# PSUM banks of a gated cross-attention layer: three for the transposed scores and two for the spare uses, in place of two and three

## The chip, the cores and the metric

The kernel runs on one core of one Trainium2 chip. The metric is the device time of one execution in microseconds (us), as the median of several executions. The engines are called TensorE (PE in the profile, with PEld for its weight loads), VectorE (DVE), ScalarE (ACT), GpSimd (POOL) and SyncE (SP, which issues most of the DMAs). PSUM, into which TensorE writes, has eight banks of 512 fp32 columns, and the kernel uses all of them.

## What is computed

One layer: gated cross-attention of 8 sequences of 112 queries on 375 context rows each, then a gated mixture of 8 feed-forward experts of which each sequence takes 3.

```
q = layernorm(x) @ Wq + bq; k = ctx @ Wk + bk; v = ctx @ Wv + bv      # 16 heads of 16
s = where(mask, -1e15, q k^T / 4); a = softmax(s) @ v; y = a @ Wo + bo
x = x + tanh(g_xattn) * y
n = layernorm(x)
p = softmax(tanh(mean(n, 1) @ W1 + b1) @ W2 + b2); w = the top 3 of 8, divided by their sum
z = n + sum over the 8 experts e of w[e] * gelu(n @ Wa[e]) @ Wb[e]
x = x + tanh(g_ffn) * z
```

## The kernel before

The engines run programs of their own, which meet in semaphores only. The attention stage is one loop over b from -2 to 7 (for TensorE lines 1244 to 1257), a pipeline over sequences: in pass b the sequence b gets its exponentials and its product with v, sequence n = b+1 its row maxima and v, sequence m = b+2 its context transposes, q and k, sequence o = b-1 its output projection, and sequence b-2 its second layernorm. After the loop comes the feed-forward stage (24 units u, three for each sequence, functions g1 and g2, lines 1267 to 1322).

A pass has four slots. In each, TensorE's program is

```python
st_tile(b, slot, 0)
s1(b + 1, 2 * slot)
st_tile(b, slot, 1)
pv(b if slot else b - 1, (slot - 1) % COUPLES)
...
st_tile(b, slot, 2)
s1(b + 1, 2 * slot + 1)
for name in uses[len(first):]:
    put(name)
```

- **st_tile(b, g, c)** (lines 1072 to 1088) computes one tile of transposed scores, keys by queries of four heads, in the bank `ST_BANKS[t % len(ST_BANKS)]` for tile number t. It is one matmul at line 1081 (maximum and mask) and two at line 1085. First it waits until the exponential of tile t - len(ST_BANKS) is done (line 1076). ScalarE's exp_tile (lines 547 to 555) reads the bank and writes pT, a ring of five tiles, for which it waits until the product pv that read the old tile is done.
- **s1(b, p)** (lines 1062 to 1070) computes the scores of two heads in banks 0 and 1 (line 1069), from which VectorE's row_max (lines 799 to 809, the instruction at line 807) takes maxima. At the first and the fifth pair it waits for q and k, which SyncE reads back from DRAM (lines 321 to 343).
- **pv(b, g)** (line 1101) multiplies by v into bank 5, and waits for the exponentials of tile (b, g, 2).
- **put(name)** is one of the spare uses, the small products of which there are 7 to 14 in a pass from b = 0 on. They take the spare banks in turn (class Spare, lines 89 to 122), and `use` (lines 1052 to 1057) waits until whoever read the last use of the same bank is done (table FREED, lines 78 to 86).

The spare uses of a full pass (2 to 5), in TensorE's order (slot_uses, lines 62 to 72):

| slot | ahead of st_tile(b, slot, 2) | behind it |
|---|---|---|
| 0 | MX1 of b, CX0 and CX1 of m | XT of m, OT of o, K0 of m |
| 1 | | K1 and Q of m, X2T of b-2 |
| 2 | MX0 of n | V0 of n, ON of o |
| 3 | | V1 of n, OP of o |

MX (line 1163) transposes row maxima, and ScalarE's max_copy (line 632) frees its bank. CX (line 1110) transposes the context; ScalarE frees CX0 (line 639) and VectorE CX1 (line 843). K0 and K1 (line 1119) are the projection of k: ScalarE's k_hi (line 655) and then VectorE's k_lo (line 849) read it, and k_lo frees the bank. Q (line 1145) is done in the same way (lines 647 and 857). X2T (line 1192) transposes the second layernorm's result: ScalarE's x2_hi (line 582) and then VectorE's x2_lo (lines 893 and 894) read it, and the last of these frees the bank; in VectorE's program x2_lo stands behind row_max(n, 5). V0 and V1 (line 1128) are the projection of v, read by ScalarE's v_copy (line 615). OT (line 1170), ON (line 1177) and OP (line 1185) belong to the output projection. X2T and what follows from it are missing where b-2 is below 0, and CX, XT, K and Q where b+2 is above 7.

ScalarE's order in a pass (lines 682 to 732) mixes these copies with the exponentials, and ends each slot with two instructions w_hi (line 665), which convert parts of the feed-forward weights; GpSimd follows them with lo_part (line 474), and only then may SyncE load further parts (lines 353 to 365) into the ring `stage`. GpSimd scales the parts that have landed (line 469) and computes the reciprocal deviation of the second layernorm (norm2, lines 479 and 480) in between; ScalarE's normed2 (line 604) waits for it, and the exponentials of slot 1 stand behind normed2 on ScalarE. SyncE's order in slot 2 is: the transposed maxima (line 350, behind max_copy of MX0), a load of weights, then k and q of m read back (lines 341 and 329).

Of the kernel before, what the change touches and what calls it, by code (L numbers as in the profile page):

```python
# [37 lines left out]
PRING = 5  # L38
ROUTES = ((0, B - 3), (B - 3, 3))
VC = HD + 1  # L40
ST_BANKS = (2, 3)
O_BANK = 5
MISC_BANKS, TAIL_BANKS = (4, 6, 7), (6, 7)


def parts_at(b, slot):
# [90 lines left out]
def need(eng, sem, n):  # L137
    if n > 0:
        eng.wait_ge(sem, n)


def flamingo_layer(nc, x, ctx, mask, g_xattn, g_ffn, Wq, bq, Wk, bk, Wv, bv, Wo, bo,
                   W1, b1, W2, b2, Wa, Wb, out):
    with ExitStack() as stack:
# [119 lines left out]
        def tile(b, g, c):  # L264
            return (b * COUPLES + g) * KC + c
# [269 lines left out]
        def _(act):  # L535
# [11 lines left out]
            def exp_tile(b, g, c):  # L547

                if there(b):
# [3 lines left out]
                    if t == 0:  # L553
                        act.wait_ge(s["zeroed"], 5)
                    a.activation(pT[0:CK, t % PRING, :], bank[0:CK, ST_BANKS[t % len(ST_BANKS)], 0:QUAD], ACT.Exp).then_inc(s["act_exp"], 1)  # L555

# [491 lines left out]
        def _(pe):  # L1048
# [23 lines left out]
            def st_tile(b, g, c):  # L1072

                if there(b):
                    t = tile(b, g, c)
                    need(pe, s["act_exp"], t - len(ST_BANKS) + 1)
                    o = bank[:, ST_BANKS[t % len(ST_BANKS)], 0:QUAD]
                    w = 128 if c < KC - 1 else CK
# [269 lines left out]
```

## Time and profile before

| | |
|---|---|
| median of 3 executions | 325.48 us (325.46 to 325.75) |
| the profiled execution | 328.27 us, its span 326.4 us |
| attention stage | up to 202.4 us of the span |
| feed-forward stage | the last 124 us |
| TensorE busy | 287.3 us, 88% of the span |
| mean granted clock of TensorE | 0.979 of full speed |

The span is what the trace covers; 1.9 us of the profiled execution lie around it. Times of rows are microseconds from the start of the span. The profiled execution took 2.8 us more than the median one.

### The profile page before, as it was taken

What the parts mean: (1) busy time and instruction counts of PE and PEld (TensorE: products, weight loads), DVE (VectorE), ACT (ScalarE), POOL (GpSimd) and SP (SyncE); (2) the same over time, 40 slices, a digit from 0 to 9 for tenths busy, and PEclk for the clock granted to TensorE, in tenths of its full rate; (3) what the DMA queues carried; (4) which work ended last, traced back from release to release, by engine and by line L of the source; (5) the groups of instructions that cost most, each with busy time, mean ns of one, the idle gap of its engine ahead of it and who ended that gap; (6) DMA issues with size and microseconds to landing.
All of it is one profiled execution on the core that took longest, in us unless ns stands there. A gap on an engine that the chain in (4) does not pass through costs nothing.

```text
span 326.4 us, 10356 instructions
## 1 busy us (share of the span) xinstructions
PE 287.3 (88%) x3940; PEld 238.6 (73%) x3940; DVE 225.3 (69%) x642; ACT 223.1 (68%) x439; POOL 135.4 (41%) x185
## 2 busy tenths in 40 slices
PE   1808769899989999999998977899999999999996
PEld 1505546667756776767765646799999989999996
DVE  7326846657757797777867626876976877686773
ACT  2221456786958968789687674986866977766863
POOL 3401274876768968689677983000100000000000
PEclk9967989999999999999999999999999999999999
DMA  7457667686777778866686322100201011010101
GB/s 166 120 125 239 156 176 213 167 241 172 233 182 216 206 230 230 264 177 172 207 217 208 88 87 80 38 19 16 58 17 46 3 44 37 11 45 3 32 2 30
DMA packets 39457, 40.59 MB, mean 124 GB/s; under 512 B 10264, under 2 KB 35264, under 8 KB 39408
## 3 DMA queue, kind: packets, MB, share of 16 engines
q1 hardware_dynamic: 37296, 38.94, 42.5%
q10 hardware_dynamic: 1936, 0.79, 1.0%
q8 instruction: 32, 0.52, 0.7%
q0 software_dynamic: 176, 0.20, 0.2%
q14 instruction: 17, 0.14, 0.1%
HBM read 33.09 MB, written 6.74 MB: 122 GB/s over the span
## 4 chain that ended last, share of the span: by engine, by line
PE 63%; DMA 12%; ACT 7%; issue 6%; DVE 5%; SPq 4%; POOL 3%; DVEq 0%; ACTq 0%
PE bank L1280 16%; PE bank L1307 16%; PE bank L1119 7%; PE bank L1128 5%; PE bank L1069 4%; DMA qbd<-q_scr 4%; PE bank L1081 4%; DMA stage<-in_L_ffn_Wb 4%; PE bank L1085 3%; PE bank L1101 2%; ACT pT L555 2%; PE bank L1110 2%; PE bank L1145 2%; DMA ctx_s<-in_ctx 2%; POOL wa L474 1%
## 5 line engine op out<-in xcount | busy, mean ns | idle before, releaser
L807 DVE CUSTOM_DVE_ANT_0 bank<-bank,maskb 112x375 f32<-112x375 f32 x128 | 67.9, 571 | 42.1 <-PE bank L1069 42.1
L1280 PE MATMUL bank<-ctxT,wqkvo 128*128 128x112 f16 x960 | 59.4, 213 | 2.7 <-DVE qbd L933 2.3
L1280 PEld LDWEIGHTS bank<-ctxT,wqkvo 128*128 128x128 f16 x960 | 56.5, 98 | 3.4 <-issue 3.4
L1307 PE MATMUL bank<-stage,pT 128*128 128x112 f16 x1104 | 58.1, 213 | 0.0
L1307 PEld LDWEIGHTS bank<-stage,pT 128*128 128x128 f16 x1104 | 55.8, 98 | 0.3
L555 ACT ACTIVATE pT<-bank 125x448 f32<-125x448 f32 x96 | 49.0, 540 | 9.9 <-PE bank L1085 9.3
L469 POOL TENSOR_SCALAR stage<-stage 128x512 f32<-128x512 f32 x64 | 38.5, 620 | 27.4 <-DMA stage<-in_L_ffn_Wa 20.6
L1069 PE MATMUL bank<-kst,qbd 128*112 128x375 f16 x128 | 33.7, 338 | 16.0 <-DMA qbd<-q_scr 12.7
L474 POOL TENSOR_TENSOR wb<-stage,wb 128x512 f16<-128x512 f32 x32 | 37.6, 1195 | 14.5 <-ACT wb L665 14.4
L1081 PE MATMUL bank<-rq,maskb 115*128 115x448 bf16 (+1 forms) x96 | 35.5, 370 | 8.3 <-ACT pT L555 7.8
L474 POOL TENSOR_TENSOR wa<-stage,wa 128x512 f16<-128x512 f32 x32 | 36.4, 1158 | 10.8 <-ACT wa L665 10.8
L1280 PE MATMUL bank<-ctxT,qbd 128*128 128x112 f16 x192 | 40.8, 213 | 0.0
L754 ACT ACTIVATE pT<-wb 128x1024 f16 x23 | 24.3, 1056 | 15.4 <-PE bank L1307 13.3
L1085 PE MATMUL bank<-qbd,kst 128*128 128x224 f16 (+1 forms) x192 | 34.4, 260 | 0.0
L932 DVE COPY wqkvo<-wa 128x3072 f16 x24 | 23.4, 973 | 15.6 <-PE bank L1280 14.2
L744 ACT ACTIVATE stage<-kst,wbc 128x448 f16<-128x448 f32 x48 | 32.1, 668 | 1.6
L1006 DVE SCALAR_TENSOR_TENSOR stage<-kst,wbc,stage 128x448 f16<-128x448 f32 x48 | 32.6, 679 | 0.6 <-ACT stage L744 0.6
L944 DVE COPY pT<-wb 128x3072 f16 x23 | 22.1, 959 | 12.5 <-PE bank L1307 12.5
L1085 PEld LDWEIGHTS bank<-qbd,kst 128*128 128x128 f16 (+1 forms) x192 | 21.6, 113 | 11.8 <-issue 1.3
L1069 PEld LDWEIGHTS bank<-kst,qbd 128*112 128x112 f16 x128 | 14.8, 132 | 21.0 <-DMA qbd<-q_scr 13.9
L742 ACT ACTIVATE kst<-bank 128x448 f32<-128x448 f32 x48 | 25.5, 532 | 2.8 <-PE bank L1280 2.8
L479 POOL TENSOR_TENSOR rstd<-ve,half 112x1 f32<-112x1 f32 x16 | 8.8, 551 | 39.8 <-DVE ve L829 39.8
(134 smaller groups left out, 480.2 us busy)
## 6 DMA issues: line engine op xcount, KB each, us to landing
stage<-in_L_ffn_Wa SPq DMA_DIRECT2D x16, 512.0 KB, 4.5
stage<-in_L_ffn_Wb SPq DMA_DIRECT2D x16, 512.0 KB, 4.5
kst<-k_scr SPq DMA_DIRECT2D x64, 93.8 KB, 3.6
k_scr<-wb SPq DMA_DIRECT2D x16, 187.5 KB
ctx_s<-in_ctx SPq DMA_DIRECT2D x8, 336.0 KB
qbd<-q_scr SPq DMA_DIRECT2D x32, 56.0 KB, 3.0
xa<-in_x SPq DMA_DIRECT2D x8, 112.0 KB, 4.1
q_scr<-wb SPq DMA_DIRECT2D x16, 56.0 KB, 3.3
```

Of the source, the lines that this page charges most:

```text
L469: g.tensor_scalar(st, st, WSCALE, 1.0, ALU.mult, ALU.mult).then_inc(s["scaled"], 1)
L474: g.tensor_tensor(part_dst(k, 1), stage[:, k % RING, :], part_dst(k, 0), ALU.subtract).then_inc(s["lo_done"], 1)
L555: a.activation(pT[0:CK, t % PRING, :], bank[0:CK, ST_BANKS[t % len(ST_BANKS)], 0:QUAD], ACT.Exp).then_inc(s["act_exp"], 1)
L742: a.activation(h_w[:, cols], bank[:, 2 * (u % 2) + hf, 0:QUAD], ACT.Gelu_apprx_tanh, scale=1.0 / WSCALE).then_inc(s["gelu_done"], 1)
L744: a.activation(hT[:, u % 2, cols], h_w[:, cols], ACT.Copy, scale=wbc[:, u:u + 1]).then_inc(s["hthi_done"], 1)
L807: v.tensor_tensor_reduce(out=bank[0:SQ, e, 0:SK], in0=bank[0:SQ, e, 0:SK], in1=maskb[0:SQ, b % 2, 0:SK], scale=-1.0, scalar=FLOOR, op0=ALU ...
L1006: v.scalar_tensor_tensor(out=hT[:, u % 2, (2 + hf) * QUAD:(3 + hf) * QUAD], in0=h_w[:, cols], scalar=wbc[:, u:u + 1], in1=hT[:, u % 2, col ...
L1069: T.matmul(bank[0:SQ, e, 0:SK], qbd[:, b % 2, e, p, :], kst[:, b % 2, p * SK:(p + 1) * SK], start=True, stop=True).then_inc(s["pe_s1"], 1)
L1081: T.matmul(o[0:w, :].rearrange("k (j q) -> k j q", j=4), maskb[0:KQ, b % 2, c * CK:c * CK + w], rq[0:KQ, g // 2, :, g % 2, :], start=True, ...
L1085: ins = T.matmul(o[0:w, i * 2 * SQ:(i + 1) * 2 * SQ].rearrange("k (e q) -> k e q", e=2), kst[:, b % 2, p * SK + c * CK:p * SK + c * CK + w ...
L1280: ins = T.matmul(o, first(ws, t, f), x2b[:, b % 2, (xs * DT + t) * SQ:(xs * DT + t + 1) * SQ], start=(t == 0 and xs == 0 and ws == 0), sto ...
L1307: ins = T.matmul(o, second(u, ws * (2 * CHUNK) + f * D + t * 128), hT[:, u % 2, hs * FT * SQ + f * SQ:hs * FT * SQ + (f + 1) * SQ], start= ...
```

## The change

The bank 7 moves from the spare uses to the transposed scores. Two constants are all that is edited. `st_tile` and `exp_tile` take the number of banks from the length of ST_BANKS, so tile t now waits for the exponential of tile t - 3 and the bank is the same as c; Spare deals the uses of the loop to the banks 4 and 6 in turn, so each waits for the use two before it, no longer for the one three before it. The uses behind the loop keep the banks 6 and 7.

```diff
-ST_BANKS = (2, 3)
+ST_BANKS = (2, 3, 7)
 O_BANK = 5
-MISC_BANKS, TAIL_BANKS = (4, 6, 7), (6, 7)
+MISC_BANKS, TAIL_BANKS = (4, 6), (6, 7)
```

What each use of a full pass waits for, by FREED, in the two versions (the kind of use whose reader frees the bank; "last" is the pass before):

| use | before | after |
|---|---|---|
| MX1 | ON, last | V1, last |
| CX0 | V1, last | OP, last |
| CX1 | OP, last | MX1 |
| XT | MX1 | CX0 |
| OT | CX0 | CX1 |
| K0 | CX1 | XT |
| K1 | XT | OT |
| Q | OT | K0 |
| X2T | K0 | K1 |
| MX0 | K1 | Q |
| V0 | Q | X2T |
| ON | X2T | MX0 |
| V1 | MX0 | V0 |
| OP | V0 | ON |

In pass 6, X2T waits for MX1 after the change and V0 for X2T; in passes 0 and 1, which have no X2T, V0 waits for Q.

## Rows read from the trace of the kernel before

**Rows 1.** TensorE's waits: engine, line, released by, us in total, times, longest.

```profile
PE bank L1069 <- DMA qbd<-q_scr: 12.7, 4, 8.3
PE bank L1081 <- ACT pT L555: 7.8, 13, 1.6
```

**Rows 2.** A stretch of 20 us: busy PE, PEld, DVE, ACT, POOL; clock; DMA share; GB/s.

```profile
109.00:129.00 20.00, 19.11 (x188) 14.01 (x176) 15.52 (x58) 16.18 (x38) 16.08 (x22) 1.00 0.77 225
```

**Rows 3.** Timeline of TensorE in pass 3: start us, us, engine, line.

```profile
109.25 0.86 PE L1110 MATMUL bank<-ident,ctx_s 125*128 125x125 f32 x6
109.95 0.35 PE L1081 MATMUL bank<-rq,maskb 115*125 115x448 bf16 x1
...
117.41 0.36 PE L1192 MATMUL bank<-ident,x 112*128 112x112 f32 x2
...
119.74 0.40 PE L1081 MATMUL bank<-rq,maskb 115*125 115x448 bf16 x1
...
120.50 1.89 PE L1128 MATMUL bank<-wqkvo,ctxT 128*125 128x256 f32 x8
...
124.89 0.40 PE L1081 MATMUL bank<-rq,maskb 115*125 115x448 bf16 x1 [0.37 <-ACT pT L555]
...
128.33 0.53 PE L1069 MATMUL bank<-kst,qbd 128*112 128x375 f16 x2 [0.42 <-DMA qbd<-q_scr]
```

**Rows 4.** Timeline of ScalarE in pass 3.

```profile
109.56 0.33 ACT L632 ACTIVATE ms<-bank 12x224 bf16<-12x224 bf16 x1
...
116.73 0.58 ACT L655 ACTIVATE wb<-bank,bk_c 128x375 f16<-128x375 f32 x1 [1.04 <-PE bank L1119]
...
122.43 0.69 ACT L615 ACTIVATE vp<-bank,vsc 125x512 f32<-125x512 f32 x1 [1.27 <-PE bank L1128]
...
124.29 0.98 ACT L555 ACTIVATE pT<-bank 125x448 f32<-125x448 f32 x2
```

**Rows 5.** Timeline of VectorE in pass 3.

```profile
117.34 0.61 DVE L849 SCALAR_TENSOR_TENSOR wb<-bank,bk_c,wb 128x375 f16<-128x375 f32 x1
...
120.53 0.56 DVE L807 CUSTOM_DVE_ANT_0 bank<-bank,maskb 112x375 f32<-112x375 f32 x1 [0.29 <-PE bank L1069]
...
121.81 0.38 DVE L894 TENSOR_REDUCE pooled<-bank 128x2 f32<-128x224 f32 x1
```

**Rows 6.** Pass 5: TensorE's CX0 and CX1 (six transposes), ScalarE's max_copy.

```profile
150.05 0.86 PE L1110 MATMUL bank<-ident,ctx_s 125*128 125x125 f32 x6
...
150.28 0.33 ACT L632 ACTIVATE ms<-bank 12x224 bf16<-12x224 bf16 x1
```

**Rows 7.** TensorE, longer waits of st_tile(b, 1, 2) in passes 2, 6 and 7.

```profile
94.39 0.40 PE L1081 MATMUL bank<-rq,maskb 115*125 115x448 bf16 x1 [1.56 <-ACT pT L555]
...
174.76 0.40 PE L1081 MATMUL bank<-rq,maskb 115*125 115x448 bf16 x1 [0.86 <-ACT pT L555]
...
193.17 0.40 PE L1081 MATMUL bank<-rq,maskb 115*125 115x448 bf16 x1 [1.36 <-ACT pT L555]
```

**Rows 8.** Pass 2: ScalarE's exponentials of slot 1, TensorE's X2T. Pass 6: V0, x2_lo's end.

```profile
93.81 0.96 ACT L555 ACTIVATE pT<-bank 125x448 f32<-125x448 f32 x2
...
97.28 0.36 PE L1192 MATMUL bank<-ident,x 112*128 112x112 f32 x2
...
179.59 0.60 PE L1128 MATMUL bank<-wqkvo,wb 128*125 128x256 f32 x2
...
180.56 0.38 DVE L894 TENSOR_REDUCE pooled<-bank 128x2 f32<-128x224 f32 x1
```

**Rows 9.** The chain that ended last, from 180 us on: start us, us, what.

```profile
183.05 2.28 POOL wa L474 x2
...
185.35 4.65 DMA stage<-in_L_ffn_Wb
...
192.60 0.53 ACT pT L555
...
197.95 4.13 DMA ctxT<-x_scr
```

## The prediction, made before the run

> **What bounds the kernel.** I read the chain that ended last first, then TensorE's waits, the busy times by stretch, and last the timelines of three engines through one pass. From 205 us on the chain is almost all TensorE in the feed-forward stage, where the change touches nothing: its banks and its spare uses are the old ones. So all is decided in the attention stage. There TensorE is busy 19.11 of 20 us in pass 3 [rows 2]: whatever it waits more, it loses, and what it waits less it wins. Its waits in the whole kernel [rows 1] name what the change aims at: 7.8 us at line 1081, st_tile waiting for ScalarE's exponential to give a score bank back. The 12.7 us for q and k from DRAM lie mostly in the first passes, before the uses have a queue. No row of before shows a wait at a spare use for its bank. With three banks that price is hidden, so it must be worked out from when each reader finishes.
>
> A semaphore from reader to TensorE costs about 0.06 us: in slot 3 of pass 3 the first of two exponentials begun at 124.29 [rows 4] (0.98 together, 0.54 the second, begun 0.44 after the first) ends near 124.83, and st_tile goes at 124.89 [rows 3].
>
> **What the third score bank gives.** In pass 3, st_tile(3, 3, 2) waited 0.37 for an exponential that stood behind weight conversions [rows 3]. That tile now needs one computed a slot earlier, so the wait goes. st_tile(3, 2, 2) at 119.74 was late by some 0.12 too, in the same way. This repeats in passes 4 and 5: a gain of 0.49 each. Longer waits stand at st_tile(b, 1, 2) in passes 2, 6 and 7: 1.56, 0.86 and 1.36 [rows 7], where ScalarE was held by the second layernorm. What is late next there is X2T, which needs that layernorm's result as well. So these go only in part (below).
>
> **What two spare banks cost.** I compare each use's start with the end of the reader that it newly waits for, in pass 3. Eleven of the fourteen find their bank free, as their readers end 0.2 us or more before, or are waited for anyway; these I cost at nothing, and what hides them is the slot of TensorE work between. Three don't:
> - CX1, the second three of six transposes issued from 109.25 to 109.95 [rows 3], would start at 109.60. MX1, just ahead, is read by ScalarE until 109.89 [rows 4], and it can't be read sooner, as two exponentials stand before it. Wait: 109.89 + 0.06 - 109.60 = 0.35. In pass 5 [rows 6] 150.61 + 0.06 - 150.40 = 0.27; I take 0.27 for pass 4 as well and 0.2 for pass 1.
> - X2T started at 117.41 [rows 3]. K1's readers are k_hi, 116.73 to 117.31 [rows 4], and k_lo, 117.34 to 117.95 [rows 5]. Wait: 117.95 + 0.06 - 117.41 = 0.60. Only Q stands between K1 and X2T and both readers follow K1 at once, so this moves with TensorE and can't be caught up. Queued behind are st_tile(b, 2, 0) and the fifth pair's scores; VectorE has other work there.
> - V0 started at 120.50 [rows 3]. Its bank is now freed by x2_lo, which VectorE ends at 121.81 + 0.38 = 122.19 [rows 5], since it stands behind row_max(n, 5), begun at 120.53 as soon as the scores arrive [rows 5]. Wait: 122.19 + 0.06 - 120.50 = 1.75. This too moves with TensorE: VectorE was idle 0.29 before that maximum. Behind V0 stand ON, the next tiles and, on ScalarE, v_copy at 122.43 [rows 4] with all that follows it: the copy of ON, two weight conversions and three exponentials. Before, V0's 1.8 us of matmuls covered x2_lo, and ON was the one to wait for it; the cover is gone.
>
> One wait for a transfer goes in return: s1 at 128.33 waited 0.42 for q [rows 3]; TensorE comes there later now, and the read doesn't move as far.
>
> **The sum.** Pass 3: 0.35 + 0.60 + 1.75 - 0.49 - 0.42 = +1.8. Passes 4 and 5: 0.27 + 0.60 + 1.75 - 0.49 = +2.1 each. Pass 1: +0.2; it has no X2T, and what its st_tiles gain in slots 2 and 3 is held back by the read of q, which follows MX0 by 8 to 9 us. Pass 0 the same, taken as nothing. Pass 2: the exponentials of slot 1 start at 93.81 [rows 8] whatever happens, as ScalarE waits for GpSimd; now the three run in a row, 0.44 apart, to 95.2, then k_hi (0.58) and k_lo (0.61) with two hops give 96.5, and X2T, which was at 97.28 [rows 8], moves 0.8 forward. CX1's 0.25 is swallowed there. Then + 1.75 - 0.49: +0.5. Pass 6: slot 1 gains about 0.8 of its 0.86 at V0, and V0 would wait 180.94 + 0.06 - 179.59 = 1.4 [rows 8]: +0.6. From V0 of pass 6 on the chain leaves TensorE: ScalarE's conversion, GpSimd (from 183.05), a load of weights of 4.65 us, the scaling, the second layernorm, the exponentials at 192.60, the routing, and the read at 197.95 that starts the feed-forward stage [rows 9]. It carries over what V0 lost, and gains 0.3 since the third exponential of slot 1 no longer waits for its tile. TensorE's 1.36 in pass 7 [rows 7] is beside that chain and worth nothing. Sum: 0.2 + 0.5 + 1.8 + 2.1 + 2.1 + 0.6 - 0.3 = +7.0 us. The profiled execution would go from 328.3 to 335.3; it stands 2.8 above the median of 325.5, so the median goes to 332.5.
>
> Bounds of what no row shows. V0's wait: at the least 1.4 per pass (the row of pass 6), at the most 1.75 and 0.5 more if ScalarE's share of x2 comes late; I take 1.75, from the nearest rows, four of five passes being alike. The hop: 0.02 to 0.1. The CX1 wait: 0 if ScalarE runs ahead, 0.5 if V0's delay leaves it behind. The gains: all 7.8 us at the upper end.
>
> **Rivals.**
> - *The bubbles are the bound, and the spare banks are not* (faster). The 7.8 us at line 1081 [rows 1] come off in full and the three waits are covered by work that I don't see. If a third of them, 3, remained: 325.5 - 7.8 + 3 = 320.7. For it: it is the only wait for a PSUM bank that the profile shows, at the same place in each pass. Against it: 3.8 of the 7.8 are the rows 7, held by the layernorm, and V0's reader ended 1.7 after V0's start in each pass. The Trainium skill, in Perfetto Trace Analysis, section Optimization Strategy, says that a gap which repeats on the engine that should be saturated can mean too little PSUM for the next tile. By that rule this rival would come true; the repeated gap of 0.37 is there, but it is the smaller of the two prices. It decides for itself if V0 finds its bank free.
> - *The transfers of q and k set the period* (slower, less). MX0 at about 119.4 releases, by SyncE's order, the read that s1 waited for at 128.33. Then only what lies ahead of MX0 counts, CX1 and X2T, and V0's wait hides beside the transfer: 5 passes by about 0.7, or +3.5: 329.0. Against it: that wait was 0.42 in pass 3 and next to nothing in the others, so it hides 1.75 nowhere.
> - *ScalarE becomes the bound* (slower still). V0's delay moves v_copy, conversions and, through GpSimd and the weight loads, the second layernorm. The holes of rows 7 then open in passes 3 to 5 too, as waits of pv or X2T: 3 by about 1.2, 7.0 + 3.6 = 10.6: 336.1. For it: ScalarE has 16.18 of 20 us of work in the pass [rows 2]. Against it: it idles 1.27 right before v_copy and 1.04 before k_hi [rows 4].
> - *Nothing is to be seen*: gains and losses cancel, 325.5. It needs V0's wait at 0.3.
>
> **How the numbers follow.** About 0.2% is what a measurement of this kernel can tell from no change. The forecast gets 0.68, with a range of its own from 330 to 334.8. The transfers get 0.11, ScalarE 0.10, the bubbles 0.08, nothing 0.03. Range: 328.8 to 335.4, which takes in the forecast, the transfers' rival and the near end of ScalarE's; the rest is left out. Faster: 0.08; same 0.03; slower 0.89.
>
> **What would show it.** In TensorE's waits, line 1081 falls from 7.8 to below 1, and new rows appear: line 1128 waiting for VectorE's line 894, 5 times, 8 us in all; line 1192 for line 849, 3 or 4 times, 2 us; line 1110 for ScalarE's line 632, 0.2 to 0.4 each. The passes 3 to 5 last 22 to 23 us instead of 20 to 21, and the feed-forward stage is as long as before and starts 7 us later. I am wrong if V0 starts right behind the sixth pair's scores, if a pass is not longer, or if VectorE or ScalarE show waits that were filled before.

## The result, and the profile after

The changed kernel takes 337.13 us (median of 4 executions) against 325.62 for the kernel before: a ratio of 1.033, 95% interval 1.023 to 1.042. It is slower, as forecast, but by 11.5 us where 7.0 was forecast, and above the range (335.4). The executions fall into two groups, two at 334.8 and 335.1, two at 339.2 and 340.0, and the median lies in the gap between them; the next runs show what parts them. The profiled execution, 334.82 us with a span of 332.9, is one of the lower group.

TensorE's waits after the change (engine, line, released by, total us, times, longest):

```profile
PE bank L1069 <- DMA qbd<-q_scr: 12.5, 4, 8.4
PE bank L1128 <- DVE pooled L894: 8.2, 5, 1.7
...
PE bank L1216 <- DVE pooled L894: 2.7, 1, 2.7
PE bank L1110 <- ACT ms L632: 2.3, 4, 0.7
...
PE bank L1192 <- DVE wb L849: 2.1, 4, 0.5
```

Line 1081, with 7.8 us the second row of [rows 1], is gone from the list. In its place stand the three waits of the forecast: V0 (line 1128) five times, X2T (line 1192) four times, CX1 (line 1110). A fourth was not forecast: W (line 1216) in pass 7 waits 2.7 us for x2_lo.

The same places of pass 4 in the timeline of TensorE, and ScalarE's max_copy and the first layernorm ahead of it, which answer to [rows 3, 4, 6]:

```profile
130.76 0.54 PE L1110 MATMUL bank<-ident,ctx_s 125*128 125x125 f32 x3
131.96 0.54 PE L1110 MATMUL bank<-ident,ctx_s 125*128 125x125 f32 x3 [0.66 <-ACT ms L632]
...
140.75 0.38 PE L1192 MATMUL bank<-ident,x 112*128 112x112 f32 x2 [0.52 <-DVE wb L849]
...
145.54 1.96 PE L1128 MATMUL bank<-wqkvo,wb 128*125 128x256 f32 x8 [1.69 <-DVE pooled L894]
...
149.41 0.40 PE L1081 MATMUL bank<-rq,maskb 115*125 115x448 bf16 x1
```

```profile
130.23 0.60 ACT L596 ACTIVATE xa<-xa,nmr,rstd 112x256 f32<-112x256 f32 x1 [0.58 <-POOL nmr L480]
130.73 0.96 ACT L555 ACTIVATE pT<-bank 125x448 f32<-125x448 f32 x2
131.58 0.33 ACT L632 ACTIVATE ms<-bank 12x224 bf16<-12x224 bf16 x1
```

V0 and X2T cost what was worked out, 1.69 and 0.52. CX1 does not: its three transposes come 1.20 us after CX0's, where in the kernel before they come 0.35 after them, so it waits 0.85 and not 0.27 (the 0.66 of the row counts only from the end of CX0's). ScalarE is late for it because it waits 0.58 for GpSimd. The tile of slot 3, at 149.41, has no wait.

How long each pass lasts, from one MX1 to the next (line 1163, read from the timelines, in us), and the last stretch from MX1 of pass 7 to the first matmul of the feed-forward stage:

| kernel | 1 | 2 | 3 | 4 | 5 | 6 | last |
|---|---|---|---|---|---|---|---|
| before | 20.1 | 21.8 | 20.7 | 20.1 | 20.3 | 18.2 | 14.1 |
| changed | 19.9 | 22.7 | 23.1 | 23.1 | 23.1 | 18.2 | 14.3 |

The sum from pass 1 on is 9.2 us more, against 7.0 forecast. The traced execution of before was in addition 2.2 us later at MX1 of pass 0 (45.85 against 43.60). This is no effect of the change, as another traced execution of the changed kernel came there at 45.14: in all three traces TensorE's granted clock is at 0.50 early on, from 19 to 29 us in those two and from 20 to 27 us in this one. The 6.55 us between the two profiled executions hide that much of the loss.

### The profile page after: what moved, and what is told of

Its sections match the earlier page's. It is cut to its first block, busy times and chain, and to the rows that moved or that the text cites. A ratio compares the mean times of both kernels' runs of the same rounds, so it can differ in the third digit from the quotient of the medians.

```text
span 332.9 us, 10356 instructions
## 1 busy us (share of the span) xinstructions
PE 287.9 (86%) x3940; PEld 237.4 (71%) x3940; DVE 224.7 (67%) x642; ACT 222.2 (67%) x439; POOL 135.1 (41%) x185
## 4 chain that ended last, share of the span: by engine, by line
PE 61%; DVE 11%; POOL 6%; ACT 6%; DMA 5%; issue 5%; SPq 3%; ACTq 1%; DVEq 0%
PE bank L1280 16%; PE bank L1307 16%; PE bank L1119 6%; PE bank L1128 4%; DVE bank L807 4%; PE bank L1069 4%; PE bank L1081 4%; POOL wa L474 3%; PE bank L1085 3%; PE bank L1101 3%; DMA qbd<-q_scr 3%; PE bank L1110 2%; POOL stage L469 2%; DVE wb L849 2%; DMA k_scr<-wb 1%
## 5 line engine op out<-in xcount | busy, mean ns | idle before, releaser
L555 ACT ACTIVATE pT<-bank 125x448 f32<-125x448 f32 x96 | 47.8, 540 | 8.4 <-PE bank L1085 7.7
L469 POOL TENSOR_SCALAR stage<-stage 128x512 f32<-128x512 f32 x64 | 38.3, 617 | 25.5 <-DMA stage<-in_L_ffn_Wa 20.7
L1069 PE MATMUL bank<-kst,qbd 128*112 128x375 f16 x128 | 33.4, 336 | 15.2 <-DMA qbd<-q_scr 12.5
L932 DVE COPY wqkvo<-wa 128x3072 f16 x24 | 23.0, 960 | 15.2 <-PE bank L1280 13.8
L1069 PEld LDWEIGHTS bank<-kst,qbd 128*112 128x112 f16 x128 | 14.9, 132 | 19.3 <-DMA qbd<-q_scr 13.4
```

The source lines that it names most:

```text
L469: g.tensor_scalar(st, st, WSCALE, 1.0, ALU.mult, ALU.mult).then_inc(s["scaled"], 1)
L1069: T.matmul(bank[0:SQ, e, 0:SK], qbd[:, b % 2, e, p, :], kst[:, b % 2, p * SK:(p + 1) * SK], start=True, stop=True).then_inc(s["pe_s1"], 1)
```

## The experiments

They were run in three groups of four, each on a chip of its own with the kernel before beside it; its medians were 325.5, 325.4 and 326.5. The changed kernel itself was timed in the first group alone, so where a run of the other two is held against it, a difference between chips (1 us for the kernel before) is in the comparison.

**The changed kernel again.** No edit.

> The changed kernel as it is, timed again beside the kernel before. Four executions of it gave 334.8, 335.1, 339.2 and 340.0 us. Theory A (the lost 9 us are new waits at spare banks, and the 4 to 5 us above them in some executions are a clock level granted in a stretch): executions fall into two groups near 335 and near 339 to 340, and the longer ones show a mean granted clock lower by 0.010 to 0.015. Theory B (all of it is one effect that varies): times spread evenly between 334 and 341 at one clock. The kernel before stays at 325.5 to 326.

Median 339.30, ratio 1.039 (1.034 to 1.044); six executions: 334.9 and five from 338.6 to 339.9. So there are two groups, and the upper one is the usual one. With the first four executions, three of ten lie at 335. The profiled execution, of 339.93 us, had a mean clock of 0.970 against 0.985, and took 17.0 us for the last stretch of the table, where the one of the lower group took 14.3. From pass 1 on its sum is 147.8 us, against 144.4 there and 135.2 in the kernel before. Its end of pass 7, and under it that of the lower group (columns: the stretch, its length, busy PE, PEld, DVE, ACT, POOL, the granted clock, DMA share, GB/s):

```profile
200.00:208.00 8.00, 4.50 (x68) 2.86 (x66) 3.79 (x14) 4.94 (x13) 6.72 (x9) 0.93 0.12 31
208.00:214.00 6.00, 6.00 (x52) 3.60 (x55) 1.49 (x3) 1.63 (x3) 0.00 (x0) 0.53 0.34 100
```

```profile
198.00:206.00 8.00, 4.52 (x66) 2.82 (x55) 3.43 (x14) 4.93 (x13) 6.28 (x8) 1.00 0.16 42
206.00:209.00 3.00, 3.00 (x56) 2.06 (x57) 1.65 (x3) 1.52 (x3) 0.00 (x0) 1.00 0.44 130
```

Both had stood still for 2.7 us ahead of W. From W to the first matmul of the feed-forward stage the one takes 6.7 us (207.69 to 214.40) and the other 4.0 (205.25 to 209.21): the lower clock costs 2.8 us there. Theory A holds.

**Two score banks and two spare banks.** The loss without the gain.

```diff
-ST_BANKS = (2, 3, 7)
+ST_BANKS = (2, 3)
```

> Two score banks as before, but only the two spare banks of the change; bank 7 is left unused. This is the loss without the gain. Theory A (the third score bank gives what the waits at line 1081 were worth, about 3 us net of what slot 1 keeps): 3 to 4 us slower than the changed kernel, 338 to 339 at the fast level. Rival (the third score bank gives nothing, because what it advances waits again at a spare bank): within 1 us of the changed kernel. Second rival (ahead of V0's wait the score waits cost nothing any more): the same.

Median 340.62, ratio 1.045 (1.041 to 1.048): 1.3 us above the changed kernel, and not 3 to 4. Theory A misses, and the rivals' 1 us is passed by a little. In the traces the third score bank is worth 0.5, 0.7 and 0.7 us in passes 1, 2 and 6 (against the profiled execution of the run above), and nothing in passes 3 to 5: here st_tile waits again in slot 3,

```profile
129.03 0.40 PE L1081 MATMUL bank<-rq,maskb 115*125 115x448 bf16 x1 [0.51 <-ACT pT L555]
```

and yet passes 3 to 5 last 23.1 us each, just as with three score banks. In the changed kernel something else sets their length. In its chain of waits the stretch from one V0 to the next CX1 does not run through TensorE:

```profile
145.54 1.98 PE bank L1128 x8
147.54 0.22 ACT vp L615
...
148.47 0.53 ACT wa L665
...
149.07 2.29 POOL wa L474 x2
151.35 1.16 POOL stage L469 x2
152.52 0.52 POOL rstd L479
153.11 0.20 POOL nmr L480
...
153.84 0.62 ACT pT L555 x2
...
154.69 0.34 ACT ms L632
155.07 0.54 PE bank L1110 x3
```

V0, v_copy, a weight conversion on ScalarE, the subtraction and the scaling on GpSimd, the layernorm behind the scaling, two exponentials, max_copy, CX1; from there TensorE and VectorE lead to X2T and the next V0. The chain is closed, and a wait removed inside a slot of TensorE only makes CX1 wait longer. With two score banks it isn't this chain that binds: ScalarE has no wait at line 596 in passes 3 to 5, and CX0 and CX1 come as one group,

```profile
132.35 0.60 ACT L596 ACTIVATE xa<-xa,nmr,rstd 112x256 f32<-112x256 f32 x1
133.47 1.15 PE L1110 MATMUL bank<-ident,ctx_s 125*128 125x125 f32 x6
```

1.15 us long in place of the 0.86 of the kernel before, so that CX1 waits some 0.3, as forecast. There TensorE's own waits, 0.3, 0.5 for X2T and 1.7 for V0, make up nearly all of the 2.7 us by which the pass is longer than in the kernel before. That both ways come to 23.1 seems to be chance.

**V0 beside MX0.** Spare banks dealt by name: V0, OP, K0, Q, XT, CX0, MX0 on one bank, the others on the other, with exceptions in the first and last passes (W beside ON in pass 7, for one).

```diff
-                    banks.append(MISC_BANKS[len(names) % len(MISC_BANKS)])
+                    banks.append(MISC_BANKS[side(name[0], b)])
```

> Three score banks and two spare banks as in the change, but the spare uses are dealt by name, so that V0 takes the bank of MX0 and no longer that of X2T. V0 then waits for a copy that is done; the waits of CX1 and X2T stay. Theory A (V0's wait of 1.7 us in five passes is the main loss, and it also delays ScalarE's weight conversion, GpSimd, the layernorm and through it max_copy, which cost CX1 another 0.5 in four passes): 8 to 10 us come back, 325 to 328 us, CX1's wait falls from 0.66 to under 0.35, and the times no longer fall into two groups. Rival (V0's wait only takes the place of another, ON's or a transfer's): under 3 us come back, 332 or more.

Median 329.47, ratio 1.012 (1.009 to 1.015): 9.8 us less than the changed kernel beside it, as theory A had it, but 1.5 above the range given for the time. All six executions lie within 1.8 us, and their mean clocks are 0.974 to 0.979: the two groups are gone, the lower clock is not. In the trace it is at 0.50 from 194 to 197 us, behind a wait of X2T of 1.62 in pass 7. V0's wait is gone; W still waits 1.0, for ON's copy. X2T still waits 0.52 four times, CX1 0.65 and 0.47 in passes 2 and 3, 0.20 in pass 5, so that part of the expectation holds only in the later ones. Passes 1 to 6 take 121.8 us in all, against 130.1 and 130.7 in the two traces of the changed kernel and 121.1 in the kernel before. The edit deals every use anew, but V0's five waits, 8.2 us, are what is gone from the list, and they are the size of the gain in those passes: V0's bank was the main loss.

**X2T in slot 2.**

```diff
-        (("K1", m), ("Q", m), ("X2T", b - 2)),
-        (("MX0", n), ("V0", n), ("ON", o)),
+        (("K1", m), ("Q", m)),
+        (("X2T", b - 2), ("MX0", n), ("V0", n), ("ON", o)),
```

> As the run before, and X2T moves from the end of slot 1 to slot 2, ahead of MX0, where K1's readers have long been done. Theory A: X2T's wait of 0.5 us in four passes goes, 2 us less than the run with V0 alone: 322.5 to 326. Rival (MX0 now comes later behind X2T, the maxima and the transfers of q and k behind it too, and a wait for q returns): within 0.5 us of that run or slower.

Median 329.15, ratio 1.010 (1.006 to 1.014): 0.3 less, so as a time the rival holds, though not by its mechanism. X2T's wait is gone and passes 1 to 6 are 1.1 us shorter in all (120.7 against 121.8). The last stretch gave it back, 16.7 against 14.9: with X2T out of the way, TensorE stood in pass 7 in one piece for the exponential behind the second layernorm,

```profile
194.90 0.36 PE L1092 MATMUL bank<-rq,maskb 115*128 115x448 bf16 x1 [2.75 <-ACT pT L566]
```

and from 200 to 204 us its granted clock was 0.58, behind a second gap, of 1.82 ahead of W.

**W apart.** In the changed kernel, W of pass 7 on ON's bank and OP on that of X2T.

```diff
-                    banks.append(MISC_BANKS[len(names) % len(MISC_BANKS)])
+                    flip = b == B - 1 and name[0] in ("W", "OP")
+                    banks.append(MISC_BANKS[(len(names) + flip) % len(MISC_BANKS)])
```

> The changed kernel with two uses of pass 7 exchanged: W takes the bank of ON, whose copy is done, and OP that of X2T. Theory A (W's wait of 2.7 us for x2_lo of sequence 5, the longest gap of TensorE late in the attention stage, is what lets its clock fall to the lower level, and with it the last slot runs at half speed in most executions): the executions near 339 become rare, the median is 334 to 336, W waits at most 1.1 us and the granted clock stays 1.00 from 180 us on. Rival (the clock falls for another reason, such as the sum of the gaps in passes 6 and 7): the median stays at 337 to 340 and a stretch with a clock below 1 remains.

Median 338.50, ratio 1.038 (1.035 to 1.042). A miss: W now waited for its own data, 2.0 us for the routing weights, and not 1.1, so the gap shrank by 0.7 only, and the clock fell all the same. The time lies where the rival had it, but as the gap stayed, this run can't part the two theories. It shows the lower clock well, behind that gap:

```profile
208.59 0.39 PE L1217 MATMUL bank<-wdiag,one 5*128 5x15 f32 x2 [2.02 <-DVE wdiag L919]
...
210.03 1.32 PE L1102 MATMUL bank<-pT,vp 125*17 125x112 f32 x24
...
212.08 1.43 PE L1186 MATMUL bank<-wqkvo,tT 128*112 128x256 f32 x4
```

The 24 products with v took 1.32, and the output projection 1.43; they take 0.77 and 1.03 at the full clock.

**The first layernorm first.** In the changed kernel, on GpSimd in slot 3.

```diff
                     ks = parts_at(b, slot)
+                    if slot == 3:
+                        norm1(b + 3)
                     for k in parts_at(b + (slot + 1) // 4, (slot + 1) % 4):
                         scale_part(k)
...
-                    if slot == 3:
-                        norm1(b + 3)
```

> The changed kernel with one move on GpSimd: in slot 3 the first layernorm's reciprocal deviation is computed ahead of the scaling of weights and no longer behind it. Theory A (in passes 3 to 5 the period is a closed chain: V0's late start delays ScalarE's weight conversion, GpSimd's subtraction and scaling, the layernorm, the exponentials behind it, max_copy and with it CX1): the wait of ScalarE's line 596 goes, CX1 waits 0.2 to 0.35 in place of 0.66 plus the gap before it, passes 3 to 5 fall from 23.1 to 22.4 to 22.7, and the whole comes out 1.5 to 3 us lower, 332 to 333.5 at the upper clock and 336 to 338 at the lower. Rival (CX1 waits for the two exponentials themselves, not for the layernorm): no change within 0.5 us.

Median 336.21, ratio 1.030 (1.026 to 1.034). Passes 3 to 5 last 22.4 us in place of 23.1, ScalarE's waits at line 596 fall from 6.4 to 2.3 us, and CX1's 0.7 in three passes are gone from TensorE's list. The time, 3.1 us below the changed kernel's 339.3 on the other chip, is in the range given for the lower clock, and the clock did fall in the trace (0.50 from 208 to 210 us). The closed chain is shown: nothing on TensorE, ScalarE or VectorE was touched. It is worth 0.7 us in a pass; the other 2.0 between 22.4 and the kernel before are of the size of TensorE's own waits at V0 and X2T (2.2).

**Two and two, the first layernorm first.** The same move with two score banks.

> Two score banks and two spare banks, with the same move on GpSimd. In the run without the move passes 3 to 5 lasted 23.1 us, just as with three score banks, although st_tile waited 0.51 in slot 3. Theory A (there the closed chain sets the period and hides what a third score bank gives; with the chain cut it shows): this kernel stands 2 to 4 us above the run with three score banks and the move, its passes 3 to 5 last 0.4 to 0.5 longer. Rival (the third score bank gives nothing anyway): within 1 us of it.

Median 340.47, ratio 1.045 (1.041 to 1.050): 4.3 us above the run with three score banks, a little more than the 2 to 4 of theory A; the rival falls. Passes 3 to 5 last 23.0 against 22.4. With the chain cut the third score bank gives 0.6 in a pass; before, 0.0. And the move, which gave 0.7 in a pass with three score banks, gives 0.1 with two: there the chain over GpSimd hardly bound.

**All three moves.** Spare banks by name, X2T in slot 2, and both layernorms first on GpSimd. The edits are those of the runs before, and on GpSimd

```diff
                     ks = parts_at(b, slot)
+                    if slot == 0:
+                        norm2(b - 2)
+                    if slot == 3:
+                        norm1(b + 3)
                     for k in parts_at(b + (slot + 1) // 4, (slot + 1) % 4):
                         scale_part(k)
-                    if slot == 0:
-                        norm2(b - 2)
...
-                    if slot == 3:
-                        norm1(b + 3)
```

> Three score banks, spare uses dealt by name (V0 beside MX0, W beside ON), X2T in slot 2, and on GpSimd both layernorms ahead of the scaling. Theory A: from the 329.2 of the same kernel without the move on GpSimd, the waits of ScalarE for the layernorms (5.6 and 6.1 us, of which some 3 on the path, in passes 2, 6 and 7) and the single wait of 2.75 us in pass 7, behind which the clock fell, go: 324 to 326.5, at or below the kernel before. Rival (the layernorm's data come late anyway, or the weights' transfers now set the pace): 328 or more.

Median 326.39, ratio 1.002 (0.999 to 1.005): level with the kernel before, as theory A had it. The sum of its passes 1 to 6 is 119.3 us against 121.1. W was late by 2.2, and after it the last slot ran at a clock of 0.66 (columns as above):

```profile
191.00:196.00 5.00, 2.81 (x40) 2.03 (x39) 3.01 (x12) 3.63 (x11) 5.00 (x5) 1.00 0.12 36
196.00:201.00 5.00, 5.00 (x61) 3.16 (x60) 1.99 (x5) 1.52 (x3) 0.18 (x1) 0.66 0.43 129
```

**A filler.** In the changed kernel, ahead of W in pass 7; it computes nothing that is used.

```diff
+                if g == 0:
+                    pe.wait_ge(s["dve_max"], s1_no(B, 0, 0))
+                    for i in range(14):
+                        T.matmul(bank[0:SQ, i % 2, 0:SK], qbd[:, 1, 1, 7, :], kst[:, 1, 7 * SK:8 * SK], start=True, stop=True)
                 pe.wait_ge(s["wdiag_done"], g + 1)
```

> The changed kernel plus 14 matmuls that compute nothing the kernel uses (scores of the last pair again, into banks 0 and 1, which are free by then), right ahead of W in pass 7, where TensorE otherwise stands still for 2.7 us. They take 2.2 us of that gap. Theory A (TensorE's idle time late in the attention stage is what lets its clock fall to the lower level, and the lower clock is 3 to 4 us of the measured loss): the stretch from 200 us on keeps a granted clock of 1.00, and the median falls from 338 to 339 to 334 to 335.5. Rival (the clock falls because of the whole light passage of passes 6 and 7, or for a reason outside TensorE's load): the median stays at 337 to 340 with a stretch at the lower clock.

Median 337.29, ratio 1.034 (1.029 to 1.039), on a chip where the kernel before took 326.5. The profiled execution kept the clock at 1.00:

```profile
203.28 2.40 PE L1217 MATMUL bank<-kst,qbd 128*112 128x375 f16 x14
206.16 0.36 PE L1220 MATMUL bank<-wdiag,one 5*128 5x15 f32 x2 [0.48 <-DVE pooled L894]
...
208.47 1.03 PE L1185 MATMUL bank<-wqkvo,tT 128*112 128x256 f32 x4
```

Its passes are those of the changed kernel, and the last stretch is 14.2 us (17.0 and 15.4 in the runs "the changed kernel again" and "W apart", where the clock fell). But the changed kernel too had one traced execution at 1.00, and this one is the fastest of six. The time misses theory A's range, 334 to 335.5, by 1.8 us and lies in the rival's. Against the changed kernel's 339.3 it is 2.0 less, or 3.0 less if the distances to the kernel before are compared (10.8 and 13.8), on different chips and with ratios whose intervals touch (1.034 to 1.044 there). Single executions still reach 340. So it isn't shown that matmuls of no use in TensorE's gap hold the clock, though all of the figures lean that way.

**W later.** All three moves, and W at the end of slot 3.

```diff
-    more = {(B - 2, 3): ("H", 0), (B - 1, 0): ("L", 0), (B - 1, 2): ("W", 0), (-1, 3): ("BO", 0)}.get((b, slot))
+    more = {(B - 2, 3): ("H", 0), (B - 1, 0): ("L", 0), (B - 1, 3): ("W", 0), (-1, 3): ("BO", 0)}.get((b, slot))
```

> The kernel with all three moves (spare uses dealt by name, X2T in slot 2, both layernorms first on GpSimd), and W moved from slot 2 of pass 7 to the end of slot 3. W waited 2.2 us for the routing weights ahead of three score tiles and the last output projection, and the clock fell behind it. Theory A: that wait leaves the path, the last slot runs at the upper clock, the feed-forward stage starts when its first transfer lands, about 199.4 in place of 201.1: 1.5 to 3 us less than 326.4, so 323.5 to 325, below the kernel before. Rival (the start of the feed-forward stage is set by the transfer and the weight copy anyway, and the clock falls as before): 326 or more.

Median 322.42, ratio 0.987 (0.983 to 0.992): the lowest of all, ahead of both kernels, and 1.1 us below the range given. The last stretch takes 12.0 us, and the clock stays at 1.00 in pass 7, with 1.22 as TensorE's longest wait there.

**The kernel before with the same two moves.** Of the edits above, the one on GpSimd and the one to `more`; the banks and the other uses stay as before.

> The kernel before (two score banks, three spare banks dealt in turn) with the two moves that don't need the change: both layernorms first on GpSimd, and W at the end of slot 3. Theory A (the third score bank is worth its 0.4 to 0.5 us in a pass once the spare uses don't wait, so the version with three score banks is ahead by 1 to 3 us): 324 to 326. Rival (the banks are worth nothing in either place and all of the gain is in the moves): within 0.5 us of the run with three score banks.

Median 322.93, ratio 0.989 (0.985 to 0.994). It is 0.5 us above the run before it, and the intervals overlap: the rival holds, and theory A's 1 to 3 us for the banks aren't there. The passes 1 to 6 take 119.7 us here and 119.9 there.

**The kernel before with the layernorms first alone.** Only the edit on GpSimd.

> The kernel before with only the layernorms first on GpSimd. Theory A (ScalarE's waits for the second layernorm, 4.9 us in passes 2, 6 and 7, lie on the path in part, as line 1081 waited 1.56, 0.86 and 1.36 behind them): 1 to 2.5 us less than the kernel before, 323 to 324.5. Rival (in the kernel before they are beside the path, which the transfers of weights set): within 0.5 us of it.

Median 324.49, ratio 0.993 (0.990 to 0.996): 2.0 us less than the kernel before, at the edge of theory A's range. The remaining 1.6 us are W's place. The traced execution, the slowest of the twelve, also shows that the lower clock doesn't need the change: with the old banks, W waited 1.77 us for its routing weights, and the clock fell behind it (0.58 in the mean of the next 4 us).

```profile
195.83 0.51 PE L1216 MATMUL bank<-wdiag,one 5*128 5x15 f32 x2 [1.77 <-DVE wdiag L918]
...
196.00:200.00 4.00, 4.00 (x37) 2.56 (x38) 1.67 (x4) 1.23 (x3) 0.00 (x0) 0.58 0.50 148
```

## Why the prediction was wrong

The direction and the mechanism were right. V0 waits for x2_lo 1.69 us five times (forecast 1.75), X2T for k_lo 0.52 four times (0.60), and line 1081 waits no more. Dealing the spare uses so that V0 finds its bank free gave back 9.8 of the 13.8 us, with W's new bank in pass 7 included. The rival of the bubbles fell: the repeated gap was closed and the kernel slowed down. The Trainium skill (Perfetto Trace Analysis, section Optimization Strategy) says only that such a gap can mean too little PSUM. The traces agree with that, as the gap went with a third bank; what fell is the step from there to a gain, since the bank was taken from uses that then waited longer. The rival of the transfers is out as well: it allowed 0.7 us in a pass, and passes 3 to 5 grew by 2.4 to 3.0.

Three steps failed.

*The term of CX1, and the gain of the third score bank.* The sum took 0.27 for CX1 in passes 4 and 5 (0.35 in pass 3), and took off 0.49 per pass for the tiles. Measured, CX1 waits 0.85, and the third score bank gives nothing at all in passes 3 to 5. Both have one cause, the chain from V0 over GpSimd's layernorm back to CX1: 0.27 would have been right with two score banks, and the 0.49 that the third one frees turn into CX1's wait. The rival "ScalarE becomes the bound" named the way (v_copy, conversions, GpSimd, the layernorm), but expected it at the second layernorm and at pv; it was the first layernorm, whose wait on ScalarE stands right ahead of max_copy. Passes 3 to 5 came out 2.4, 3.0 and 2.8 us longer and not 1.8, 2.1 and 2.1. Of the 9.2 us against 7.0, this is 2.2. The other terms were off singly and cancelled, which is luck: pass 2 came to 1.0 (0.5 in the sum), pass 1 to -0.1 (0.2), pass 6 to 0.0 (0.6), the last stretch to 0.2 (-0.3).

*W, costed at nothing.* The prediction counted the fourteen uses of a full pass, and took all of TensorE in pass 7 as beside the chain. There W waits for x2_lo of sequence 5, which VectorE does after the routing, and everything of slot 3 is queued behind W. The bank is only the last part of that wait, though. In the changed kernel VectorE ends W's own data at 204.50 and x2_lo at 205.11,

```profile
203.85 0.65 DVE L918 TENSOR_TENSOR wdiag<-wz,ident 5x15 f32<-5x15 f32 x1
204.44 0.37 DVE L893 TENSOR_TENSOR x2T<-bank,x2T 128x224 f16<-128x224 f32 x1
204.74 0.37 DVE L894 TENSOR_REDUCE pooled<-bank 128x2 f32<-128x224 f32 x1
```

so 0.6 of the 2.7 us are the bank's, and with another bank W still waited 2.0. In the kernel before it waited 1.05 for the same data:

```profile
197.98 0.39 PE L1216 MATMUL bank<-wdiag,one 5*128 5x15 f32 x2 [1.05 <-DVE wdiag L918]
```

TensorE had been held in pass 7 at two tiles before that, for 1.36 and 0.48, and the third score bank takes these two waits away; it then stands at W in one piece. At the full clock all this cost little, as pass 7 had slack (the last stretch 14.3 against 14.1).

*The clock.* The prediction took the durations as given. In the usual execution of the changed kernel the clock falls to the lower of its two levels, 1.2 GHz, late in pass 7, behind TensorE's longest gaps, and its matmuls take up to twice as long: 2.8 us from W on, by the two traces of this kernel. The kernel before had its gaps of 1.36 and 1.05 there and kept 1.00 in its trace. Without the fall, the executions near 335 lie just inside the range, so the clock is what took the median out of it. In the traces the loss from pass 1 on is 9.2 us with the clock held and 12.5 with the fall (147.8 against 135.2); the six executions timed together gave 13.8, the four first ones, half of them in the lower group, 11.5. The remaining 1.3 us aren't settled. Executions of one kernel differ by more than that before pass 1, as the two traces of the changed kernel do.

## What to carry to other kernels

Uses that share banks in turn are priced by the reader that now stands closest: list for each use, in all passes and the short last ones too, when its new predecessor's reader ends. Before a removed wait is counted as a gain, look for a closed chain over the other engines that keeps the period, and behind each new long gap of TensorE read the granted clock. And try the order of work first: two moves that need no bank gave 3.6 us (322.9 against 326.5), and the third score bank on top of them, with the spare uses dealt by name and X2T moved, nothing that could be measured (322.4).

## What the runs showed of the hardware

TensorE's clock fell from 1.00 to 0.50 in pass 7 behind gaps of 1.6 to 2.7 us, in a stretch in which it was busy about half the time (4.50 of 8 us in the changed kernel, 2.81 of 5 in the run with all three moves), and not always: the changed kernel met the same gap of 2.7 us in two traced executions, once with the clock held at 1.00 and once with the fall. It fell with the old banks too, behind 1.77 us. Gaps of 1.7 us in passes where it was busy 20 of 23 us never cost the clock in any trace, nor did the gaps of 1.36 and 1.05 of the kernel before or the 1.22 of the run with W later. What in the gap decides is open. At the lower clock the 24 products with v took 1.32 us in place of 0.77.
